# Indexed gathers of a recommendation tower: let go one by one instead of in three groups per half

## The reference

```
e = stack([tbl_f[ids[:, f]] for f in range(16)], axis=1)          # (2048, 16, 16)
A  = repeat(e, 39 copies along axis 1)    Bm = repeat(r_x0, ...)   # both (2048, 624, 16)
z = einsum('bnh,bnd,nk,khd,kd->bkh', A, Bm, alpha, w, hv)         # (2048, 16, 16)
h = concat([z.reshape(2048, 256), dense_ctx], axis=1)
h = max(h @ W_top1 + b_top1, 0); h = max(h @ W_top2 + b_top2, 0); y = h @ W_top3
```

## Time and profile before

| | us |
|---|---|
| median of 3 runs | 196.21 (194.47 to 199.51) |
| span of the profiled execution | 296.9 |
| busy in it: PE, DVE, POOL, ACT | 226.7, 153.7, 116.6, 76.1 |
| gathers (L420), 116 | 116.4, mean 1003 ns |
| products (L509), 40 | 91.2, mean 2283 ns |

### The profile page before, as it was taken

One profiled execution on the slowest core, in us unless ns is written; L12 is line 12 of the kernel. 1 busy time (PEld: TensorE's weight loads), 2 busy tenths in 40 slices (PEclk: granted clock), 3 DMA queues, 4 the chain that ended last, 5 costly groups with the idle time before them and its releaser, 6 DMA issues.

```text
span 296.9 us, 6045 instructions
## 1 busy us (share of the span) xinstructions
PE 226.7 (76%) x2630; PEld 156.7 (53%) x2630; DVE 153.7 (52%) x173; ACT 76.1 (26%) x212; POOL 116.6 (39%) x120
## 2 busy tenths in 40 slices
PE   6221676989698569969692989889697796699996
PEld 2200564447377328646451866657466564347774
DVE  5500291086869349544480494929628673066900
ACT  3500350271422140306000350314023022022322
POOL 4777017100636361723446034634561737400000
PEclk9999995559779897968897797979759997569999
DMA  6976205000779715640255046460544334000000
GB/s 180 258 168 188 121 2 121 2 3 3 183 264 304 273 10 143 223 151 2 59 116 205 0 146 148 139 234 6 147 149 145 78 76 148 6 2 0 2 0 2
DMA packets 14579, 32.72 MB, mean 110 GB/s; under 512 B 6499, under 2 KB 10448, under 8 KB 11472
## 3 DMA queue, kind: packets, MB, share of 16 engines
q1 hardware_dynamic: 9717, 29.95, 32.4%
q0 software_dynamic: 3712, 0.96, 3.3%
q10 hardware_dynamic: 1124, 1.43, 1.6%
HBM read 32.28 MB, written 0.05 MB: 109 GB/s over the span
## 4 chain that ended last, share of the span: by engine, by line
PE 49%; another core or an unknown queue 14%; issue 7%; ACT 4%; DVE 0%; ACTq 0%
PE bank L773 14%; PE bank L706 10%; PE bank L700 9%; PE bank L728 8%; PE bank L761 3%; PE bank L693 3%; ACT tower L546 2%; ACT e_cols L569 1%; PE bank L714 1%; PE bank L752 1%; PE bank L686 0%; ACT tower L548 0%; ACT ids_b L540 0%; ACT tower L602 0%
## 5 line engine op out<-in xcount | busy, mean ns | idle before, releaser
L420 POOL DMA_INDIRECT e<-tbl_dram,ids_all x116 | 116.4, 1003 | 139.9 <-DVE prod L509 104.2
L509 DVE TENSOR_TENSOR prod<-x,bank 128x2048 f32<-128x2048 f32 x40 | 91.2, 2283 | 59.9 <-issue 30.5
L437 DVE TENSOR_SCALAR onehot<-ids_b 125x2304 bf16<-125x2304 f16 (+5 forms) x90 | 51.5, 621 | 21.4 <-PE bank L728 20.3
L728 PE MATMUL bank<-parts,onehot 125*128 125x48 bf16 x1248 | 45.6, 189 | 22.2 <-issue 20.4
L728 PEld LDWEIGHTS bank<-parts,onehot 125*128 125x128 bf16 x1248 | 40.6, 100 | 31.4 <-issue 27.2
L773 PE MATMUL bank<-prod,m_w 128*32 128x256 f32 x640 | 52.4, 431 | 4.6 <-issue 3.6
L700 PE MATMUL bank<-tower,w_z 128*128 128x256 f32 x128 | 39.5, 457 | 6.0 <-ACT tower L602 5.6
L706 PE MATMUL bank<-tower,w 128*128 128x256 f32 x128 | 36.9, 429 | 6.2 <-ACT tower L546 4.5
L773 PEld LDWEIGHTS bank<-prod,m_w 128*32 128x32 f32 x640 | 22.0, 122 | 27.2 <-issue 20.1
L700 PEld LDWEIGHTS bank<-tower,w_z 128*128 128x128 f32 x128 | 27.4, 226 | 14.4 <-ACT tower L602 8.3
L706 PEld LDWEIGHTS bank<-tower,w 128*128 128x128 f32 x128 | 26.7, 220 | 13.7 <-ACT tower L546 6.6
(11 more groups left out here) (47 smaller groups left out, 86.9 us busy)
## 6 DMA issues: line engine op xcount, KB each, us to landing
x<-x_dram SPq DMA_DIRECT2D x16, 1024.0 KB
x<-x_dram SPq DMA_DIRECT2D x16, 512.0 KB
ids_b<-ids_half_dram SPq DMA_DIRECT2D x4, 576.0 KB
e<-tbl_dram,ids_all POOLq DMA_INDIRECT x116
prod<-windows_c_dram ACTq DMA_DIRECT2D x1, 768.0 KB
prod<-windows_c_dram ACTq DMA_DIRECT2D x1, 512.0 KB
w_z<-w_z_dram SPq DMA_DIRECT2D x1, 512.0 KB
w<-w_dram SPq DMA_DIRECT2D x1, 512.0 KB
```

The costliest lines, as they stand in the source:

```text
L420: nc.gpsimd.indirect_dma_start(out=e[:, tile, f * D:(f + 1) * D], out_offset=None, in_=t[f"tbl_{f}"][:, :], in_offset=bass.IndirectOffsetO ...
L437: nc.vector.tensor_scalar(onehot[:, at % NPLANE, lo:hi, :], ids_b[0:TP, n % 2, lo:hi, :], float(k), None, ALU.is_equal).then_inc(hot_made, 1)
L509: nc.vector.tensor_tensor(prod[:, s % NPROD, :].rearrange("p (q b) -> p q b", q=HP), x0[:, tile % NX, :].rearrange("p (q b) -> p q b", q=H ...
L728: made = nc.tensor.matmul(out, onehot[:, PLANE_AT[n, lo, k] % NPLANE, j, bt * P:(bt + 1) * P], parts[:, KT_AT[f] + k, :, :], start=k == 0 ...
```

## The change

The three thresholds `GATHERS_AFTER` go. A new table `BESIDE` gives every single gather of the halves 1 to 7 its own wait. Step g of the half before lets go the gathers from number g·14//5 up to (g+1)·14//5 (of 14; of 18 for the last half): two, three, three, three, three. The first of them waits until the product of that step is made (`prod_made`), the second until the first plane of that step is made (`hot_made`), the third and any further until its last plane is made; where a step has no planes, all wait for the product. Order and number of the gathers, their destinations and semaphores stay, and so does the program of every other engine.

```diff
+def _beside():
+    found = {}
+    for n in range(1, NH):
+        of_half = sum(2 * len(fs) for fs in GATHERED[n])
+        for g in range(UH):
+            s = UH * (n - 1) + g
+            planes = [PLANE_AT[n_hot, lo, k] + 1 for n_hot, lo, hi, k in PLANES.get(s, [])]
+            marks = [("prod", s + 1)] + ([("hot", planes[0]), ("hot", planes[-1])] if planes else [("prod", s + 1)] * 2)
+            for i in range(g * of_half // UH, (g + 1) * of_half // UH):
+                found[n, i] = marks[min(i - g * of_half // UH, 2)]
+    return found
+
+
+BESIDE = _beside()
...
-GATHERS_AFTER = [-1, 1, 2]
...
+                at = 0
                 for j in range(3):
-                    if UH * (n - 1) + GATHERS_AFTER[j] > 0:
-                        pool.wait_ge(prod_made, UH * (n - 1) + GATHERS_AFTER[j])
                     for f in GATHERED[n][j]:
                         for tile in range(2 * n, 2 * n + 2):
+                            if n > 0 and BESIDE[n, at][0] == "prod":
+                                pool.wait_ge(prod_made, BESIDE[n, at][1])
+                            elif n > 0:
+                                pool.wait_ge(hot_made, BESIDE[n, at][1])
```

More of the change, by code:

```diff
@@ L423, in _ @@
                             ).then_inc(gathered[n][j], 16)
+                            at += 1
         @block.vector
```

## The result

The changed kernel takes 205.0 us (median of five runs, 204.2 to 210.3) against 196.1 us before: a ratio of 1.045, with a 95% interval of 1.041 to 1.049. It is slower, by 8.9 us. The forecast was 199.5. Some executions of a kernel run at a lower granted clock and take longer (the profiled one of after is among them, at 0.909, where the three shortest of the five have 0.95 and spans of 202.1 to 202.9); the ratios here compare the undisturbed executions alone, the medians take in all of them, so the two can differ by a per cent.

What follows compares the result with a forecast made beforehand. PE, DVE and POOL were taken as level at about 18.3 us per middle half, none with room. From 196.2 us, 3.0 for late group 0 and 0.3 for the last half gave 199.5 us, range 191.5 to 206.

Steps and rivals of the forecast that it cites:

- the likeliest case: Whole kernel: late gathers make it slower, 199.5 us against 196.2, own range 197 to 203; chance 0.47.
- Within 2%: Whole kernel: measured time about the same as before, chance 0.45 (0.29 from the forecast's case, 0.16 from no effect).
- The three engines are level: Middle halves: PE 18.3 us, DVE 18.2 and POOL 18.2 per half, none with room; whole kernel 197.4 us.
- (e): Last half: eighteen gathers wait for step 30's product, windows ready 26.0 us behind it, PE there at 25.9; cost 0.3 us.
- (a): POOL's waits: 102 where it had 20; taken as costing nothing.
- the first rival: Middle halves: POOL becomes the bound, with gathers slowed beside planes and lost time not caught up; 208 us, chance 0.20.
- (b): Start: six gathers of half 1 no longer run there, at about 22 to 29 us; costs nothing.
- (c): First windows of halves 2 to 6: group 0 comes late, PE stalls 0.6 us each; 3.0 us (0 to 14).
- T: Time mark: the end of the product of step 2 of the half before; spread forecast done at T + 5.7.
- (d): Groups 1 and 2 of each half: late release covered by other work, up to a landing time of 6 us.
- second rival: Gather bursts starve PE in timed runs too, so breaking them up gives time back; 190 us, chance 0.17.
- What would show it: Profile after: no 12 us stretch with 28 matmuls; ACT waits for gathers at step 3 of halves 1 to 5, PE for ACT.

Runs made afterwards that it cites:

- second profile of before: The kernel before, unchanged, profiled once more: 198.8 us, with a profiled span of 196.7 us.
- e3: The changed kernel with every gather's wait two steps earlier: 196.8 and 198.0 us (1.002 and 1.012 times before); 292.3 us beside 291.2 with the chip in the slow condition.
- e2: The kernel before with the change's single waits for the last half alone: 204.2 us, 1.026 times before.
- e1: The changed kernel with the old waits put back for the last half's 18 gathers alone: 208.9 us, 1.058 times before.
- e5: The changed kernel without waits for each half's first six gathers: 206.7 us; 296.7 and 296.3 us with the chip in the slow condition.

## Why the prediction was right or wrong

The direction of the likeliest case was right and the size wrong: 3.3 us of loss were forecast, 8.9 measured. "Within 2%" had got more chance (0.45) than "slower" (0.38).

**The three engines are level.** Right. In the second profile of before PE is busy for 91% of the span and POOL runs without a break through the second half of it. The whole, 197.4 us from pieces at full rate, is within 1 us of the 196.7 us span, but by luck, as the pieces cancel: up to the sixth product 57.0 were taken and 55.3 measured, for the five halves to step 30 91.5 and 96.6 (half 1 takes 23.0, the others 18.2 to 18.6), from step 30 to step 35 19.5 and 15.4, from there to the end 29.4 both times. The third of these is the piece that goes wrong in (e).

**Waits and overlap with planes cost nothing** (a, and the first rival). Right for (a). POOL's mean gather is 1026 ns after and 1031 before. In the trace of after the 56 gathers that overlap a `tensor_scalar` of DVE take 1.11 us on average and the 60 others 0.94, in the second one of before 58 and 58 with 1.12 and 0.94: as many lie beside planes, and they lose as little. The first rival, POOL bound by slower gathers, had the right engine and the wrong mechanism: POOL is the bound after the change because it starts late, at an unchanged rate. Its price (208 us) was nearer than the forecast's.

**Six gathers leave the start: nothing** (b). Right where PE isn't starved (19.9 and 20.4 us to the first product), wrong where it is, by 8 us at the first product.

**Group 0 lands late** (c). The mechanism is there, as ACT waits for gathers in front of the first windows of all five halves, but the term was built from two wrong times that cancel. Landing, where I had expected to be wrong most easily, took 4.9 to 7.0 us for the last gather of group 0 in these halves, where 4.3 were taken (the median of 3.5 in the page of after is that of all gathers), and so the windows are ready 6.1 to 9.1 us behind T and not 5.7. PE comes to the transposes 7.0 to 8.9 us behind T in the second profile of before and not 5.1. So it waited once for ACT, 1.0 us in half 5, in place of 0.6 in each half; with the slower matmuls behind it that is the 3.2 us of the profile, and that this is near the term of 3.0 is luck. With four gathers less at the end the loss shrank to 0.8%, so in timed runs the term is worth some 1.5 us (0.2 to 2.8). Where PE is hit, it is hit twice, by the wait and by the clock behind it, which the term left out.

**Groups 1 and 2 are covered** (d). Right for the middle halves, as far as the profile shows.

**The last half** (e). This is the step that failed. The time of the gathers' side came out right: windows ready 26.0 us behind the product of step 30, against 183.57 - 157.28 = 26.3. But POOL didn't start there at that product, as I had it: it was still at work on half 6 and came 1.5 us later, and the rest was that much shorter than taken, as the landing (2.3 us from the last gather's start) already holds that gather's own time. PE's side was wrong. I had it arrive 25.9 us behind that product, by taking one stall of 8.5 us out of a stretch of the starved profile; the rest of that stretch was slow too. Unstarved, in the second profile of before, the product of step 30 ends at 154.1 and PE comes to the transposes at 175.85, 21.8 us behind it; in that of after it is ready at 179.17, 21.9 us behind. The difference from 26.3 is the idle time of 4.4 us in front of them. Its price also left out the clock: 2.5 us on the work behind it. So the term of 0.3 us (bounds 0.1 to 4) measured 6.9 in the profile and 5 to 6 in timed runs (5 with the last half alone changed, 6 between the changed kernel and the one with four gathers less, which were timed apart).

**The stalls of the first profile in timed runs** (second rival). I had ruled most of it out by a sum, and for the runs that were compared this holds, though the sum was right by luck. But the stalls aren't made by the profiler: a profile of the same kernel has them or not (spans of 296.9 and 196.7 us), and in three comparisons the kernel before took 292 us. There the rival was right in its sign (281 us against 292). That the length of the later bursts brings the gain is not borne out by e3; a part arises at the start.

**What would show it.** ACT's waits at step 3 of halves 1 to 5 are all there, PE's behind them only in one. No 12 us stretch with 28 matmuls is in the profile after, but neither is one in the second profile of before, so that sign told nothing of the change.

## What to carry to other kernels

An engine that is busy for as long as the loop takes can't catch up: if its work is let go later, everything it still has to do moves by as much, and the place to look at is the last piece with the most work, not the average one. Ask from which event on the engine runs without a break, count all the work that it has left there, that of earlier pieces too (24 gathers here, not 18), add its serial time, and compare with when the result is needed. Putting back one part of such a change doesn't test it while earlier work in the same queue is still held up. And before subtracting stalls from a profile that is far longer than the timed runs, profile the same kernel once more: a total that comes out right doesn't prove its pieces.

## What the runs showed of the hardware

The same program on the same kind of chip took 196 us in some comparisons and 292 in others, with PE getting on by a few matmuls at a time while POOL's gathers ran (28 in 12 us). It is no effect of the profiler, as profiles of one kernel exist with it and without it, and it turned a loss of 4.5% into a gain of 1 to 3%.

A gather took 2.3 us from its start to landing with no loads under way (180.04 to 182.34, the chain above), and 7.0 beside `x0` loads (125.59 to 132.59 on the same chain). A gather beside a `tensor_scalar` of DVE took 1.11 us on average, one without 0.94.

An idle time of 4.4 us on PE was followed by 2.5 us of loss on a lower clock (0.5 of full speed, 1.2 GHz), and idle times of 3.8 us (e2) and 4.2 us (e1) in the same place by the same 3.62 us for eight matmuls of `l2` in place of 1.89. Behind 2.9 us (e5) they took 2.85.
